# Rows turned by VectorE after a trip through HBM, in place of 296 TensorE transposes

## The chip, the cores and the metric

The kernel runs on one core of a Trainium2 chip. The metric is device microseconds (us) of one execution; lower is better. The kernel before takes 2199.61 us, the median of three runs (2198.78 to 2200.4).

## The reference, cut to what matters

The input is 1250 rows of 1024 values. Everything below is in fp32.

```python
xn = layernorm(x)                                    # no scale, no shift
u  = xn @ root + bias + sum_r mean_r(xn) @ weight[r]  # 8 relations, 40000 edges
z  = concat([u, xn]) @ w_gate + b_gate
h  = tanh(u) * z + xn * (1 - z)
q, k, v, g = xn @ Wq, xn @ Wk, xn @ Wv, sigmoid(xn @ Wg + bg)     # 16 heads of 64
o  = linear_attention(elu(q) + 1, elu(k) + 1, v) * g
x1 = x + h + o @ Wo
i, c, f = layernorm(x1) @ W_iT + b_i, ... @ W_cT + b_c, ... @ W_oT + b_o   # one LSTM step from zero
out = x1 + sigmoid(f) * tanh(sigmoid(i) * tanh(c))
```

Four matrices of 1250 x 1024 serve as the left factor of products and are needed with their columns on the partitions: `xn`, `o`, `u` and `layernorm(x1)`, in this order.

## The kernel before, in words

The rows are cut into ten tiles of 128 (the last has 98). A product by one half (512 columns) of a weight matrix is a *stage*, one tile of it a *unit* (`UNIT`, `STAGE`, `place`): 24 matmuls, eight steps `k` over the contraction by three, since each operand is split into a high part (fp32r) and the rest. The stages in order are 16 of `weight` (Y), then R, V, K, X, G, Q, O, C and the three of the last layer (I, T, F), mostly two of each. Units are named here as C1,4: stage C, half 1, tile 4. In the first two stages tiles alternate between the halves, so tile t (up to 5) is wanted at unit 2t. Q has 12 units of another shape a half, O, C and I ten.

Nothing is scheduled automatically. Each of the five engines has one program written in order, a loop over the units `q` and the steps `k`, with semaphores between them. What an engine's code does "at step k of unit q" stands in that place of its own queue; a wait there holds back everything after it on that engine. The SyncE queue (SP) issues all the loads and stores that are named here. Its loop for unit q begins while TensorE is at unit q-1, since it ends with `store_unit(q-1)`, which waits until the result of unit q-1 is out of PSUM. There are three accumulators (`acc`): unit q can't begin before the result of q-3 is taken (by ScalarE in Y and V, by VectorE's `evict`, `elu_high` or `make_x1` elsewhere). In stage Q TensorE also waits, at step 5 of each unit, for VectorE's `elu_high` of the unit before (`read_out`).

A left factor is turned tile by tile beside the products. For `xn`, `turn_x` at the units of `TURN_AT`; for `o`, `turn_o` at `TURN_O_AT`; for `u`, `turn_u` two units behind O1; for `layernorm(x1)`, `turn_x1` three units behind C1. Each is eight TensorE transposes of 128 x 128 into the PSUM tile `tp` at k = 2 (L821; tile 0 of x by L829), then at k = 4 ScalarE's copy to the high part `aThi` (L991) and at k = 5 VectorE's subtraction to `aTlo` (L1148). The tile must be there when the first stage that uses it comes to it.

`ln_x` normalizes a tile of x on VectorE (L1155 to L1170) at the units of `LN_AT`; GpSimd's `rows_sum` adds it to x (L1671); SP stores both (`xn_d`, `xs_d`, L726, L728), and loads the next tile of x into the place that falls free (`next_x`, L520), four places in all. In C1, `make_x1` (L1519 to L1530) makes a tile of x1 and its sums, ScalarE takes the root, `scale_x1` makes the scale, and ScalarE's `normalize_x1` (L1036) writes the normalized halves to `A` and `lnb`.

Of the kernel before, what the change touches and what calls it, by code (L numbers as in the profile page):

```python
# [199 lines left out]
def build(nc, x, src, dst, edge_type, weight, root, bias, w_gate, b_gate, Wq, Wk, Wv, Wg, bg, Wo,  # L200
          W_iT, b_i, W_oT, b_o, W_cT, b_c, out):
    with ExitStack() as ctx:
# [308 lines left out]
        def _(sp):  # L511
# [1340 lines left out]
```

## Time and profile before

| | before |
|---|---|
| median of 3 runs | 2199.61 us |
| profiled execution | 2199.8 us, of which span 2198.0 us |
| TensorE (PE) busy | 2182.2 us, 99% of the span |
| VectorE (DVE) busy | 1177.1 us, 54% |
| ScalarE (ACT) / GpSimd (POOL) busy | 439.9 us / 718.6 us |
| chain that ended last | PE 98%, of it L821 (transposes) 1% and L968 90% |
| granted TensorE clock | full, in all 40 slices |
| DMA | 416.62 MB, mean 190 GB/s |

The span is the time between the first and the last instruction. Matmuls overlap in the profile: one is shown as 0.39 to 0.40 us long while the next begins 0.23 us later, so starts are what to read.

### The profile page before, as it was taken

What the parts mean: (1) busy time and instruction counts of PE and PEld (TensorE: products, weight loads), DVE (VectorE), ACT (ScalarE), POOL (GpSimd) and SP (SyncE); (2) the same over time, 40 slices, a digit from 0 to 9 for tenths busy, and PEclk for the clock granted to TensorE, in tenths of its full rate; (3) what the DMA queues carried; (4) which work ended last, traced back from release to release, by engine and by line L of the source; (5) the groups of instructions that cost most, each with busy time, mean ns of one, the idle gap of its engine ahead of it and who ended that gap; (6) DMA issues with size and microseconds to landing.
All of it is one profiled execution on the core that took longest, in us unless ns stands there. A gap on an engine that the chain in (4) does not pass through costs nothing.

```text
span 2198.0 us, 25434 instructions
## 1 busy us (share of the span) xinstructions
PE 2182.2 (99%) x10042; PEld 1768.3 (80%) x10042; DVE 1177.1 (54%) x1605; ACT 439.9 (20%) x618; POOL 718.6 (33%) x597
## 2 busy tenths in 40 slices
PE   8999999999999999999999999999999999999999
PEld 6878888888888888888777787889988888888887
DVE  6331677726666566665765676653432367234233
ACT  3221111211111111100221200112321314121121
POOL 4103002055555555544655355521210453000000
PEclk9999999999999999999999999999999999999999
DMA  7543321456788988784968788853127885013102
GB/s 254 186 131 97 110 85 50 128 199 204 274 284 289 312 294 311 243 265 140 324 230 312 241 296 297 273 178 129 48 78 232 270 284 169 34 35 120 59 35 80
DMA packets 191266, 416.62 MB, mean 190 GB/s; under 512 B 33951, under 2 KB 44772, under 8 KB 191146
## 3 DMA queue, kind: packets, MB, share of 16 engines
q1 hardware_dynamic: 127946, 229.10, 30.8%
q0 software_dynamic: 63200, 185.89, 25.4%
q8 instruction: 79, 1.29, 0.2%
q14 instruction: 41, 0.34, 0.1%
HBM read 352.34 MB, written 103.66 MB: 207 GB/s over the span
## 4 chain that ended last, share of the span: by engine, by line
PE 98%; DVE 1%; DMA 0%; ACT 0%; issue 0%; DVEq 0%; ACTq 0%
PE acc L968 90%; PE acc L963 5%; PE tp L821 1%; PE agg L872 1%; PE misc L857 1%; DVE Wlo L1143 0%; DMA xr<-in_x 0%; PE agg L976 0%; PE acc L976 0%; DVE stats L1155 0%; PE tp L829 0%; PE misc L872 0%; DVE xnb L1170 0%; ACT L1012 0%; DVE aTlo L1148 0%
## 5 line engine op out<-in xcount | busy, mean ns | idle before, releaser
L968 PE MATMUL acc<-Whi,aThi 128*128 128x512 f32 (+1 forms) x2872 | 1138.1, 396 | 2.1 <-DVE Wlo L1143 1.6
L968 PE MATMUL acc<-Whi,aTlo 128*128 128x512 f32 (+1 forms) x2872 | 1131.8, 394 | 0.0
L968 PE MATMUL acc<-Wlo,aThi 128*128 128x512 f32 (+1 forms) x2872 | 1128.3, 393 | 0.0
L968 PEld LDWEIGHTS acc<-Whi,aTlo 128*128 128x128 f32 (+1 forms) x2872 | 532.6, 185 | 133.5
L968 PEld LDWEIGHTS acc<-Wlo,aThi 128*128 128x128 f32 (+1 forms) x2872 | 533.8, 186 | 130.9
L968 PEld LDWEIGHTS acc<-Whi,aThi 128*128 128x128 f32 (+1 forms) x2872 | 532.5, 185 | 132.4 <-DVE Wlo L1143 2.0
L1708 POOL DMA_INDIRECT ring<-y_d,edge x390 | 485.1, 1244 | 428.4 <-DVE U L1339 159.1
L1143 DVE TENSOR_TENSOR Wlo<-Wraw,Whi 128x1024 fp32r<-128x1024 f32 x152 | 186.8, 1232 | 322.3 <-ACT Whi L987 321.9
L999 ACT COPY res<-acc 128x512 f32<-128x512 f32 (+1 forms) x180 | 105.8, 588 | 833.8 <-PE acc L968 810.8
L1339 DVE SCALAR_TENSOR_TENSOR U<-ring,edge,U 128x1024 f32<-128x1024 f32 x180 | 230.3, 1280 | 23.2 <-DMA ring<-y_d,edge 22.8
L1339 DVE SCALAR_TENSOR_TENSOR odd<-ring,edge,odd 128x1024 f32<-128x1024 f32 x170 | 217.5, 1279 | 22.2 <-DMA ring<-y_d,edge 21.8
L987 ACT CAST Whi<-Wraw 128x1024 fp32r<-128x1024 f32 x152 | 158.5, 1046 | 196.2 <-DMA Wraw<-in_L_gnn_w_gate 71.9
L1469 DVE TENSOR_TENSOR res<-acc,bias_sb 128x512 f32<-128x512 f32 x99 | 68.5, 691 | 213.2 <-PE acc L968 123.4
L1695 POOL DMA_INDIRECT slot_d<-table,slot x20 | 21.8, 1088 | 227.9 <-DVEq L1299 222.4
L1045 ACT ACTIVATE res<-res 128x512 f32<-128x512 f32 (+1 forms) x59 | 37.3, 633 | 282.3 <-DVE res L1469 282.3
L1448 DVE SCALAR_TENSOR_TENSOR res<-acc,res 128x512 f32<-128x512 f32 (+3 forms) x44 | 28.0, 637 | 103.9 <-ACT res L1012 103.9
L1148 DVE TENSOR_TENSOR aTlo<-tp,aThi 128x1024 fp32r<-128x1024 f32 (+1 forms) x39 | 46.7, 1198 | 53.7 <-ACT aThi L991 53.7
L963 PE MATMUL acc<-aThi,Whi 128*128 128x384 f32 (+1 forms) x192 | 69.9, 364 | 0.0
L1815 POOL TENSOR_TENSOR og<-og,part 128x384 f32<-128x384 f32 (+1 forms) x32 | 27.7, 876 | 127.8 <-DVE part L1499 127.8
L963 PE MATMUL acc<-aThi,Wlo 128*128 128x384 f32 (+1 forms) x192 | 67.6, 352 | 0.0
L963 PE MATMUL acc<-aTlo,Whi 128*128 128x384 f32 (+1 forms) x192 | 67.5, 352 | 0.0
L1010 ACT ACTIVATE res<-acc 128x512 f32<-128x512 f32 (+3 forms) x44 | 24.5, 556 | 181.2 <-PE acc L968 93.0
(177 smaller groups left out, 1034.8 us busy)
## 6 DMA issues: line engine op xcount, KB each, us to landing
y_d<-res SPq DMA_DIRECT2D x144, 256.0 KB
Wraw<-in_L_gnn_weight SPq DMA_DIRECT2D x64, 512.0 KB, 5.5
Wraw<-in_L_gnn_w_gate SPq DMA_DIRECT2D x16, 512.0 KB, 6.0
ring<-y_d,edge POOLq DMA_INDIRECT x390, 6.3
xr<-in_x SPq DMA_DIRECT2D x9, 512.0 KB, 4.5
xn_d<-xnb SPq DMA_DIRECT2D x9, 512.0 KB, 5.6
xs_d<-xr SPq DMA_DIRECT2D x9, 512.0 KB, 5.6
ur_d<-res SPq DMA_DIRECT2D x18, 256.0 KB
```

Source lines behind the costliest of these rows:

```text
L963: mm = nc.tensor.matmul(to, a[:, s % 2, k, cols], b[:, k, c0:c0 + w], start=start, stop=stop)
L968: mm = nc.tensor.matmul(to, a[:, k, rows(i)], b[:, s % 2, k, :], start=start, stop=stop)
L987: nc.scalar.copy(granule(Whi, n), granule(Wraw, n)).then_inc(w_hi, 1)
L999: nc.scalar.copy(res[0:width(i), q % 3, :], acc[0:width(i), q % 3, :]).then_inc(evac_a, 1)
L1045: nc.scalar.activation(a, a, ACT.Tanh if kind == T_ else ACT.Sigmoid).then_inc(gate_act, 1)
L1143: nc.vector.tensor_tensor(granule(Wlo, n), granule(Wraw, n), granule(Whi, n).bitcast(F32), ALU.subtract).then_inc(w_lo, 1)
L1148: nc.vector.tensor_tensor(aTlo[:, :, rows(t)], turned_rows(width(t)), aThi[:, :, rows(t)].bitcast(F32), ALU.subtract).then_inc(done, 1)
L1339: nc.vector.scalar_tensor_tensor(to, g, scale, to, ALU.mult, ALU.add).then_inc(u_acc, 1)
L1448: nc.vector.scalar_tensor_tensor(a, p, 0.0, a, ALU.max, ALU.add).then_inc(evac_v, 1)
L1469: nc.vector.tensor_tensor(to, p, bias_sb[0:w, n % 2, :], ALU.add).then_inc(evac_v, 1)
L1708: pool.indirect_dma_start(ring[:, j % RING, :], None, a, bass.IndirectOffsetOnAxis(ap=index, axis=0), bounds_check=top - 1, oob_is_err=Fal ...
L1815: nc.gpsimd.tensor_tensor(o, o, part[0:w, a % 2, n, :], ALU.mult).then_inc(gated, 1)
```

## The change

The transposes of `o`, `u`, `layernorm(x1)` and of tiles 3 to 9 of `xn` leave TensorE. The rows are stored to HBM and read back by quarters: partition 32a + n gets, of the rows n, n+32, n+64, n+96 of the tile, the columns of quarter a (256 of them). VectorE's transpose of 32 x 32 blocks then gives 128 columns on the partitions, in another order of the contraction than before; the host stores the weights in the same order. `aTraw`, the target, lies over `aTlo`, and is subtracted in place.

- `load_quarters`: a tile is 4 loads of 128 KB in pieces of 1 KB, 8 loads for the last tile. It serves `xn` (`load_z`), `o` (`load_o`), `u` (`load_u`), `layernorm(x1)` (`load_x1n`), and `xn` again for tanh(u) (`load_tx`). `store_th` stores by quarters.
- New stores: `store_o` (three groups of tiles), `store_x1n` (two halves a tile). `xn` was stored before.
- VectorE: `turn_quarters` at k = 2 or 3, one instruction a tile (two for the last), and `rows_sum` in place of GpSimd's; for tiles 0 to 2, which TensorE still turns, a copy ahead of it.
- The places: `LN_AT`, `TURN_AT`, `XS_AT`, `NEXT_X_AT`; `turn_u` one unit behind, `turn_x1` four.

```diff
-LN_AT = {1: 2, 2: 3, 4: 4, 6: 5, 7: 6, 8: 7, 9: 8, 10: 9}
-TURN_AT = {1: 1, 3: 2, 5: 3, 7: 4, 8: 5, 9: 6, 10: 7, 11: 8, 12: 9}
+LN_AT = {1: 2, 2: 3, 5: 4, 6: 5, 7: 6, 8: 7, 10: 8, 11: 9}
+TURN_AT = {1: 1, 3: 2, 5: 3, 7: 4, 8: 5, 9: 6, 10: 7, 12: 8, 13: 9}
+TURNED_BY_PE = 3
+XS_AT = {4: (0,), 5: (1, 2, 3), 6: (4,), 7: (5,), 8: (6,), 9: (7,), 11: (8,), 12: (9,)}
+NEXT_X_AT = {5: (0,), 6: (1, 2, 3), 8: (4,), 9: (5,)}
-TURN_O_AT = {place(Q_, 1, 6 + t): t for t in range(3)}
-TURN_O_AT |= {place(Q_, 1, 10): 3, place(Q_, 1, 11): 4, place(O_, 0, 0): 5}
-TURN_O_AT |= {place(O_, 0, t - 4): t for t in range(6, T)}
+TURN_O_AT = {place(Q_, 1, 7 + t): t for t in range(3)}
+TURN_O_AT |= {place(Q_, 1, 11): 3, place(O_, 0, 0): 4, place(O_, 0, 1): 5}
+TURN_O_AT |= {place(O_, 0, t - 3): t for t in range(6, T)}
+STORE_O_AT = {place(Q_, 1, 6): 0, place(Q_, 1, 10): 1, place(O_, 0, 2): 2}
+        aTraw = at(top[0] - up(4 * K * N), "aTraw", [128, K, N])
         def u_turn(q):
-            return turn_at(O_, 1, 2, q)
+            return turn_at(O_, 1, 1, q)
+        def x1_norm(q):
+            return turn_at(C_, 1, 1, q)
         def x1_turn(q):
-            return turn_at(C_, 1, 3, q)
+            return turn_at(C_, 1, 4, q)
+            def load_quarters(to, of, t, done):
+                for a in range(4):
+                    part = to[32 * a:32 * a + 32, :].rearrange("p (m f) -> p m f", f=QUARTER)
+                    cols = slice(a * QUARTER, (a + 1) * QUARTER)
+                    if t < T - 1:
+                        sp.dma_start(part, blocks(of[rows(t), cols])).then_inc(done, 16)
...
+            def load_z(t):
+                sp.wait_ge(xn_st[t % XS], 16 * (t // XS + 1))
...
+                load_quarters(zx[:, t % 2, :], xn_d, t, z_in[t % 2])
+            def store_o(g):
+                sp.wait_ge(gated, reads_to(12 + 4 * g + 3))
+                sp.dma_start(o_d[g * 384:g * 384 + 384, :].rearrange("(t p) n -> p t n", p=128), og[:, 3 * g:3 * g + 3, :]
+                             ).then_inc(rows_st, 16)
...
+            def load_o(g):
+                sp.wait_ge(rows_st, 16 * (4 if g == 2 else g + 1))
+                if g:
+                    sp.wait_ge(o_turned, 3 * g)
+                for t in group_tiles(g):
+                    load_quarters(og[:, t, :], o_d, t, o_in)
+            def store_x1n(t):
+                sp.wait_ge(ln2_done, 2 * (t + 1))
...
+            def load_x1n(t):
+                sp.wait_ge(rows_st, 16 * 4 + 32 * (t + 1))
...
+                load_quarters(zx1[:, t % 2, :], x1n_d, t, z_in[t % 2])
             for q in range(UNITS + 1):
+                if LN_AT.get(q - 2, 0) >= TURNED_BY_PE:
+                    load_z(LN_AT[q - 2])
+                if LN_AT.get(q - 1, 0) >= TURNED_BY_PE:
+                    store_xn(LN_AT[q - 1])
+                for t in XS_AT.get(q, ()):
+                    if t < TURNED_BY_PE:
+                        store_xn(t)
+                    store_xs(t)
+                for t in NEXT_X_AT.get(q, ()):
+                    next_x(t)
...
                     store_unit(q - 1)
...
+                if x1_norm(q - 3) is not None:
+                    load_x1n(x1_norm(q - 3))
+                if x1_norm(q - 2) is not None:
+                    store_x1n(x1_norm(q - 2))
+            def turn_quarters(of, t, done):
+                of = of.rearrange("p (m j f) -> p j m f", m=4, f=32)
+                if t < T - 1:
+                    nc.vector.transpose(aTraw[:, :, rows(t)], of).then_inc(done, 1)
...
+            def turn_o(t):
+                g = min(t // 3, 2)
+                dve.wait_ge(o_in, 16 * sum(quarter_transfers(p) for p in range(group_tiles(g).stop)))
+                dve.wait_ge(prod, place(Q_, 1, 4 * g + 3) + 1)
+                turn_quarters(og[:, t, :], t, o_turned)
```

Three places show how the work moved. The first is VectorE in the early units, tiles 3 and 4 of x: before, from the high part of tile 2 on (`tp` is the PSUM tile).

```order
L1148 TENSOR_TENSOR aTlo<-tp,aThi 128x8x128 [waits x_hi]
L1155 BN_STATS stats<-xr 128x6 [waits x_in0]
...
L1170 TENSOR_SCALAR xnb<-xr,stats 128x1024 [waits xs_made,x_turned,xn_st0,dve_step]
L1148 TENSOR_TENSOR aTlo<-tp,aThi 128x8x128 [waits x_hi]
L1155 BN_STATS stats<-xr 128x6 [waits x_in1]
```

The same place now (`zx` holds the quarters of xn):

```order
L1297 TENSOR_TENSOR xr<-xr,xnb 128x1024 [waits ln_done]
L1303 BN_STATS stats<-xr 128x6 [waits x_in0]
...
L1317 TENSOR_SCALAR xnb<-xr,stats 128x1024 [waits xs_made,xn_st0,dve_step]
L1297 TENSOR_TENSOR xr<-xr,xnb 128x1024 [waits ln_done]
L1266 STREAM_TRANSPOSE aTraw<-zx 128x8x128 [waits z_in1]
L1260 TENSOR_TENSOR aTlo<-aTraw,aThi 128x8x128 [waits x_hi]
L1303 BN_STATS stats<-xr 128x6 [waits x_in1]
```

Before, the transposes of tile 3 stood on TensorE; now the turn of tile 3 stands on VectorE behind the normalization of tile 4, which waits for the load of tile 4 of x (`x_in0`).

The second place is SP in the same units, now:

```order
L832 DMA xn_d<-xnb 128x1024 [waits ln_done]
L624 DMA y_d<-res 128x512 [waits evac_a]
L574 DMA zx<-xn_d 32x4x256 [waits xs_made,x_turned,xn_st3]
L574 DMA zx<-xn_d 32x4x256 x3
L832 DMA xn_d<-xnb 128x1024 [waits xs_made]
L837 DMA xs_d<-xr 128x1024 [waits xs_made]
...
L837 DMA xs_d<-xr 128x1024 [waits xs_made] x2
L567 DMA xr<-in_x 128x1024 [waits xs_st0]
L624 DMA y_d<-res 128x512 [waits evac_a]
L832 DMA xn_d<-xnb 128x1024 [waits ln_done]
L837 DMA xs_d<-xr 128x1024 [waits xs_made]
L567 DMA xr<-in_x 128x1024 [waits xs_st1]
```

The first load of `xr` is that of tile 4, behind six stores of rows and the quarters of tile 3; the load of tile 5 stands behind the store of the normalized tile 4.

The third place is SP in C1, now (`zx_139` is the buffer `zx1`, `x_d` the array of x1):

```order
L748 DMA cring<-base_d 128x512
L624 DMA x_d<-res 128x512 [waits x1_made]
L574 DMA zx_139<-x1n_d 32x4x256 [waits x1_turned,rows_st]
L574 DMA zx_139<-x1n_d 32x4x256 x3
L756 DMA x1n_d<-A 128x512 [waits ln2_done]
L757 DMA x1n_d<-lnb 128x512
L748 DMA cring<-th_d 128x512 [waits res_st2,x1_made]
```

The quarters of one tile are loaded behind the store of the unit's x1 (`x1_made`), so behind VectorE's work on the same unit. VectorE there, now:

```order
L1673 TENSOR_TENSOR res<-acc,cring 128x512 [waits p_made,prod,ln2_done,res_st0]
L1675 TENSOR_TENSOR res<-res,cring 128x512 [waits evac_v]
L1677 BN_STATS x_stats<-res 128x6 [waits x1_made]
...
L1266 STREAM_TRANSPOSE aTraw<-zx_139 128x8x128 [waits prod,z_in0]
L1690 RECIPROCAL x_scale<-x_scale 128x1 [waits ln2_root]
...
L1260 TENSOR_TENSOR aTlo<-aTraw,aThi 128x8x128 [waits x1_hi]
L1673 TENSOR_TENSOR res<-acc,cring 128x512 [waits p_made,prod,ln2_done,res_st1]
```

One unit's result is taken (L1673), then the transpose waits for the quarters (`z_in0`), the scale for ScalarE's root, the subtraction for ScalarE's high part, and only then is the next result taken. ScalarE in the same units, now:

```order
L1135 ACTIVATE lnb<-res,x_scale 128x512 [waits x1_turned,ln2_ready]
L1135 ACTIVATE A<-A,x_scale 128x512
L1122 ACTIVATE x_scale<-x_scale 128x1 [waits ln2_var]
L1091 CAST aThi<-aTraw 128x8x128 [waits x1_turned]
L1135 ACTIVATE lnb<-res,x_scale 128x512 [waits x1_turned,ln2_ready]
```

The rows are the same as before in kind, but the turn that `normalize_x1` (L1135) of tile t waits for, that of tile t-2, now stands one unit behind it in VectorE's queue; before it stood in TensorE's queue, in the unit of the normalization itself.

## Rows read from the trace of the kernel before

**Rows 1.** Page, busy time: engine, us, share of the span, instructions.

```profile
PE 2182.2 (99%) x10042; PEld 1768.3 (80%) x10042; DVE 1177.1 (54%) x1605; ACT 439.9 (20%) x618; POOL 718.6 (33%) x597
```

**Rows 2.** Chain that ended last, around the last turn of o: start, us, what.

```profile
1635.22 0.88 PE tp L821 x8
...
1641.66 0.87 PE tp L821 x8
1642.54 5.57 PE acc L968 x24
1648.11 0.68 PE tp L821 x8
```

**Rows 3.** Groups by line: busy us, mean ns, idle before.

```profile
L821 PE MATMUL tp<-ident,A 128*128 128x128 f32 x36 | 5.4, 273 | 0.8 <-DVE aTlo L1148 0.8
```

**Rows 4.** Timeline of TensorE, turn of tile 3 of x: start, us.

```profile
44.91 1.03 PE L821 MATMUL tp<-ident,xnb 128*128 128x128 f32 x8
```

**Rows 5.** Timeline of VectorE, early units; in brackets idle us before, releaser.

```profile
30.58 1.28 DVE L1170 TENSOR_SCALAR xnb<-xr,stats 128x1024 f32<-128x1024 f32 x1
41.40 1.29 DVE L1155 BATCH_NORM_STATS2 stats<-xr 128x6 f32<-128x512 f32 x2 [5.16 <-DMA xr<-in_x]
44.23 0.81 DVE L1170 TENSOR_SCALAR xnb<-xr,stats 128x1024 f32<-128x1024 f32 x1
```

**Rows 6.** Timeline of SP's queue, early units.

```profile
36.77 0.43 SPq L520 DMA_DIRECT2D xr<-in_x  x1
40.71 0.50 SPq L728 DMA_DIRECT2D xs_d<-xr  x1
47.50 0.33 SPq L520 DMA_DIRECT2D xr<-in_x  x1
57.12 0.46 SPq L728 DMA_DIRECT2D xs_d<-xr  x1
62.12 0.33 SPq L520 DMA_DIRECT2D xr<-in_x  x1
```

**Rows 7.** A window in O1: us, engines busy, clock, DMA share, GB/s.

```profile
1700.00:1720.00 20.00, 20.00 (x102) 16.54 (x101) 8.01 (x8) 6.86 (x7) 7.19 (x3) 1.00 0.96 345
```

**Rows 8.** The loads of V in pieces of 512 bytes, by tile.

```profile
L565 SPq DMA_DIRECT2D vld<-v_d x20: 348/360/605, 1073.3 to 1252.0; - x20
...
DMA to landing us min/median/max: 2.8/3.8/6.9
```

**Rows 9.** Page, groups: VectorE's pass over 1024 values in SBUF.

```profile
L1143 DVE TENSOR_TENSOR Wlo<-Wraw,Whi 128x1024 fp32r<-128x1024 f32 x152 | 186.8, 1232 | 322.3 <-ACT Whi L987 321.9
```

**Rows 10.** Timelines of GpSimd, ScalarE and VectorE in Q1.

```profile
1570.67 1.01 POOL L1815 TENSOR_TENSOR og<-og,part 128x384 f32<-128x384 f32 x1 [3.86 <-DVE part L1499]
1581.89 0.49 ACT L1010 ACTIVATE res<-acc 128x384 f32<-128x384 f32 x1 [2.82 <-PE acc L963]
1583.04 0.56 DVE L1448 SCALAR_TENSOR_TENSOR res<-acc,res 128x384 f32<-128x384 f32 x1 [1.64 <-ACT res L1012]
1586.45 0.56 DVE L1499 TENSOR_TENSOR part<-agg,rden 128x384 f32<-128x384 f32 x1
```

**Rows 11.** Timeline of VectorE, first result of C0.

```profile
1753.41 0.69 DVE L1519 TENSOR_TENSOR A<-acc,cring 128x512 f32<-128x512 f32 x1 [10.95 <-POOL cring L1826]
```

**Rows 12.** Timelines of VectorE and ScalarE in C1.

```profile
1811.80 0.69 DVE L1519 TENSOR_TENSOR res<-acc,cring 128x512 f32<-128x512 f32 x1
1812.52 0.94 DVE L1521 TENSOR_TENSOR res<-res,cring 128x512 f32<-128x512 f32 x1
1818.97 1.16 DVE L1521 TENSOR_TENSOR res<-res,cring 128x512 f32<-128x512 f32 x1
...
1815.92 0.82 ACT L1036 ACTIVATE lnb<-res,x_scale 128x512 f32<-128x512 f32 x1 [0.16 <-DVE x_scale L1540]
1816.64 0.80 ACT L1036 ACTIVATE A<-A,x_scale 128x512 f32<-128x512 f32 x1
1821.43 1.03 ACT L987 CAST Whi<-Wraw 128x1024 fp32r<-128x1024 f32 x1
1822.37 1.01 ACT L991 CAST aThi<-tp 128x1024 fp32r<-128x1024 f32 x1
```

More of the change, by code:

```diff
@@ L367, in build @@
             sem(n) for n in ("ln_var", "ln_root", "ln_done", "xs_made", "x_turned", "x_hi", "x_lo"))
+        z_in = [sem(f"z_in{i}") for i in range(2)]
+        z_turned = sem("z_turned")
+        rows_st = sem("rows_st")
+        o_in = sem("o_in")
         edges_in, edges_made, tail_made, codes_st, samples_in = (
@@ L441, in with_halves, with quarter_transfers, quarters_in, x_quarters_in @@
             return t + 2
+        def quarter_transfers(t):
+            return 8 if t == T - 1 else 4
+        def quarters_in(t, places):
+            return 16 * sum(quarter_transfers(p) for p in range(t % places, t + 1, places))
+        def x_quarters_in(t):
+            return 16 * sum(quarter_transfers(p) for p in range(t, TURNED_BY_PE - 1, -2))
+        def blocks(a):
+            return a.rearrange("(m n) f -> n m f", n=32)
         def x_tiles(i):
@@ L638, in store_th @@
                     wait_th_stored(sp, t - TH_SEMS)
-                sp.dma_start(th_d[rows(t), :], uio[t][0:width(t), :]).then_inc(th_st[t % TH_SEMS], 16)
+                done = th_st[t % TH_SEMS]
+                for a in range(4):
+                    part = uio[t][32 * a:32 * a + 32, :].rearrange("p (m f) -> p m f", f=QUARTER)
+                    cols = slice(a * QUARTER, (a + 1) * QUARTER)
+                    if t < T - 1:
+                        sp.dma_start(blocks(th_d[rows(t), cols]), part).then_inc(done, 16)
+                    else:
+                        sp.dma_start(blocks(th_d[t * 128:t * 128 + 96, cols]), part[:, 0:3, :]).then_inc(done, 16)
+                        rest = N - t * 128 - 96
+                        sp.dma_start(th_d[N - rest:N, cols],
+                                     uio[t][32 * a + 32 - rest:32 * a + 32, 3 * QUARTER:4 * QUARTER]).then_inc(done, 16)
             def load_u(t):
@@ L834, in turn_x @@
                 pe.wait_ge(x_lo, with_halves(t - 1))
[L835 removed]
+                for j in range(K):
+                    tr = turn_step(t, j)
+                tr.then_inc(x_turned, 1)
             def any_bad():
@@ new lines, in turn_x1, with rows_sum @@
+            def turn_x1(t):
+                dve.wait_ge(z_in[t % 2], x_quarters_in(T - 2 + t % 2) + quarters_in(t, 2))
+                dve.wait_ge(prod, place(C_, 1, t) + 1)
+                turn_quarters(zx1[:, t % 2, :], t, x1_turned)
+            def rows_sum(t):
+                dve.wait_ge(ln_done, with_halves(t))
+                if t < TURNED_BY_PE:
+                    chain(nc.vector.tensor_copy(by_quarters(xnb[:, t, :]), by_steps(zx[:, t % 2, :])))
+                a = xr[0:width(t), t % XS, :]
+                nc.vector.tensor_tensor(a, a, xnb[0:width(t), t % XS, :], ALU.add).then_inc(xs_made, 1)
@@ L1599, in _ @@
                         continue
+                    if k == 2 and TURNED_BY_PE <= TURN_AT.get(q, 0):
+                        turn_x(TURN_AT[q])
                     if k == 4 and q in TURN_AT:
-                        lo_turned(TURN_AT[q], x_hi, with_halves(TURN_AT[q]), x_lo)
-                    if k == (4 if q == 1 else 0) and q in LN_AT:
+                        lo_x(TURN_AT[q])
+                    if k == 4 and q == 1:
+                        rows_sum(0)
+                    if k == (4 if q in (1, 8, 10) else 0) and q in LN_AT:
                         ln_x(LN_AT[q])
+                        if q >= 3:
+                            rows_sum(LN_AT[q])
+                    if k == 4 and q == 3:
+                        for t in range(1, 4):
+                            rows_sum(t)
                     if q == 17 and k == 6:
```

198 lines of the change are left out of this document (113 added, 85 removed).

## The prediction, made before the changed kernel was run

> **What bounds the kernel now.** I read the page first: TensorE is busy 99% of the span [rows 1], at full clock in all slices, so only what shortens or delays TensorE's own queue counts. The chain of waits shows what the change can win: a unit of 24 matmuls takes 5.57 us, and where a tile is turned, 0.87 or 0.88 us stand between two such pieces, 0.68 for the last tile of 98 rows [rows 2]. Then I read the engines that come in for TensorE, place by place: VectorE and SP's queue in the early units [rows 4 to 6], VectorE and GpSimd in Q1 and C0 [rows 10, 11], VectorE and ScalarE in C1 [rows 12]. VectorE's 54% says little here: what matters is how long one of its instructions waits for a transfer while results that TensorE needs taken stand behind it.
>
> **What is removed.** 37 turns leave TensorE: 33 of full tiles at 0.87 and four of last tiles at 0.68, 28.7 + 2.7 = 31.4 us, and 0.8 us in which it waited for VectorE before a turn of x1 [rows 2, 3]. Sum: -32.2 us. Nothing covers this time now, so it is won wholly, if nothing else comes late.
>
> **Prices of what is added.** SP's issue of a load or store: 0.33 to 0.50 us [rows 6], taken as 0.45. From the issue of a 512 KB store to the wait behind it: 5.0 us (57.12 to 62.12) and 6.8 us (40.71 to 47.50). From the issue of a load of x to its use: 4.6 us (36.77 to 41.40) [rows 5, 6]. For a load of 128 KB there is no row; the nearest are 256 KB loads in pieces of 512 bytes, 2.8 to 3.8 us [rows 8], bounded below by the data alone at 345 GB/s, 0.4 us [rows 7]. I take 3.3. VectorE's transpose of 1024 columns isn't in the trace: its nearest passes are 0.81 us (one operand) and 1.23 us (two) [rows 5, 9]; I take 1.2, with 0.8 and twice the longer one, 2.45, as ends. ScalarE's high part stays at 1.0 us [rows 12].
>
> On transfers the Trainium skill has a rule, in "DMA: Bandwidth & Descriptors", § Anatomy of one DMA: about 2.0 us fixed and the bytes at 436 GB/s, as fitted for GpSimd's path. As an estimate by it a quarter lands after 2.3 us, 1.0 sooner than the value I take, so that each of some eight steps of C1 would be 1 us shorter and the sum 8 us smaller; the rows of V contradict it, with a least value of 2.8 us. On the transpose "VectorE: DVE Perf Modes", § The three transpose paths, gives 311 ns for 128 x 128 in bf16; eight of them would be an estimated 2.5 us a tile, for which I have no row.
>
> **The early units.** Tile 3 of x is wanted at unit 6. TensorE gets there at 44.91 + 0.87 + 18 x 0.232 = 49.96 before [rows 4], so at 49.1 without the turn. VectorE's queue now has: normalize tile 4, add it to x, turn tile 3. Tile 4 needs its load, and that stands in SP's queue behind a chain: tile 3 is normalized at 31.9 before [rows 5], now 2.0 later for the copy and the sum of tile 0 (0.8 + 1.2), 33.9; its store lands 5.0 later, 38.9; then four quarters and a store, and `xs_d` of tile 0, to 41.1; that lands at 46.1; the load issued then takes 4.6 if alone, 50.7. It isn't alone: quarters, stores of rows and units that are issued between 39 and 46 make 4.5 MB, at 345 GB/s 13 us, to 52; with the load's own 1.5 us and 2 of landing 55.5. I take 54 between 50.7 and 55.5. From there: normalize 41.40 to 45.04, 3.6 us [rows 5], sum 1.2, turn 1.2, high part 1.1, low part 1.2, together 8.3, to 62.3 against 49.1: +13.2 (10 to 15).
>
> Tile 4 is wanted two units later, 62.3 + 11.1 = 73.4. The load of tile 5 is issued when tile 4 is normalized and summed, 54 + 3.6 + 1.2 and three issues, 60; it lands at 64.6; two tiles are normalized and summed in VectorE's queue ahead of this turn (2 x 4.8), then 3.5 for turn, high and low part: 77.7, so +4.3 (0 to 6). Tiles 8 and 9 have the same pattern with a unit or two of reserve; +1.5 (0 to 3.5). Early units: +19 (10 to 25).
>
> **Q1 and O0.** The first group of o is complete at 1571.7 [rows 10]. Its store is 1.5 MB: 5.0 to 6.8 for the first third and 2.9 for the rest at 345 GB/s, 8.5, to 1580.2. Then 12 quarters: 11 issues of 0.45 and 3.3, to 1588.4. VectorE comes to the turn at 1583.6 - 0.9 = 1582.7 and waits 5.7 us. Behind it stand high and low part, `attend` (1.0) and the `elu_high` of Q1,7: 1588.4 + 1.2 + 1.1 + 1.2 + 1.0 + 0.6 = 1593.5. TensorE wants that at step 5 of Q1,8, which begins at 1581.9 - 0.9 + 4.9 = 1585.9, so at 1589.2: +4.3. I count 3.5, since the middle of the store's row is a guess, and as much again for the second and third group together, whose turns meet SP's queue in the same state, but behind a unit more. +7 (2 to 12).
>
> **C0.** The first result of C0 is taken 10.95 us late already [rows 11], and the next of its kind would stop TensorE 2 us later. It hangs on the last tile of tanh(u), whose load is now eight transfers behind four stores by quarters. No turn is left to give it time: +2 (0 to 4).
>
> **C1.** From C1,4 on, VectorE takes a result and adds (0.7 and 0.7 to 1.2 [rows 12], 1.6); SP stores x1 and issues four quarters (0.37 + 3 x 0.45 to the last issue, then 3.3: 5.0); turn 1.2; ScalarE normalizes the tile that waits for this turn (0.72 + 0.80), takes the root (0.2) and makes the high part (1.0, with 0.9 for a weight's in every other unit) [rows 12], 2.7 and 0.45 on average; low part 1.15. That is 12.1 us a step where a unit is 5.57. If the bn sums and the scale fall wholly into these waits nothing is added for them. Counted from below (landing 2.8, adding 0.7, no weight) it is 10.9; I take 11.3, nearer the lower end, because the first tiles' normalizations wait for no turn. TensorE, three accumulators ahead, needs the result of C1,9 at the start of I0,2: after 6 steps and 0.7, 68.5, where 8 units are 44.6: +23.9. The next takes a step more and a unit, +5.7. Then the steps have no x1 to make, but tile 7's rows are stored one step late: +4. C1 and I0: +34 (22 to 45).
>
> Work that moved and costs nothing: GpSimd's sums ran beside all else, and VectorE's ten (12 us) are paid in the early chain alone, where I counted them; quarters of u are loaded up to six tiles ahead. In O1 SP has 14 issues (6.3 us) in a unit of 5.57 for four units, 3 us of arrears that `xs` and stores, two units ahead, cover. The DMA share there is 0.96 already [rows 7], and the same bytes in pieces of 1 KB keep the rate only if a piece costs no more than its bytes; no row shows that, and a rival below has it.
>
> **Sum.** -32.2 + 19 + 7 + 2 + 34 = +29.8. The profiled execution took 2199.8 us, so 2229.6; the median of the runs is 0.2 lower: 2229.4 us. By ends: -32.2 + 34 = 2201.4 and -32.2 + 86 = 2253.4.
>
> **Rivals.** *All rows come in time.* For it: TensorE is the one bound, VectorE is idle 46% of the span, and there are three accumulators. It decides if a step of C1 is under (44.6 - 0.7)/6 = 7.3 us and tile 4 of x lands by 41 as before. Then 2199.6 - 32.2 = 2167.4. Against it: a store and a load in series alone are 10 us in the early chain, and 5 of each step are SP's queue and one landing. 6 in 100, with all below 2190.
>
> *The lower ends hold together*, stores landing in 5.0 and quarters in 2.8 wherever they are waited for: 2190 to 2212, centre 2201. 12 in 100.
>
> *VectorE's transpose is slow or small pieces are.* A transpose of 2.45 adds 1.25 in about 13 places on the path (two early, three in Q and O, eight in C1): +16, 2245. If pieces of 1 KB also take more of the DMA engines' time, O1, full now, falls behind, and quarters land later in every chain. 2248 to 2280, 20 in 100.
>
> **How the numbers follow.** The forecast has 62 in 100, with a range of its own of 2212 to 2248. To hold 8 in 10 I take in part of the slow rival and the lower end's upper half: 2206 to 2262. A measurement can tell about 0.2% (4.4 us) from no change. Faster: the first rival's 0.06 and 0.02 of the second. Same: 0.03. Slower: 0.89.
>
> **What would show each step.** No transposes of og, uio, A and lnb on TensorE, and units of 5.57 us there. TensorE idle some 13 us before unit 6 and some 4 before unit 8, released by VectorE's `aTlo`; VectorE idle there on the load of x, and in C1 on the quarters, with results taken 11 us apart for six units; TensorE idle 5 to 6 us before each of several units of C1 and I0. If VectorE shows no wait on the quarters in C1 longer than 2 us, or x's tile 4 lands before 45, the forecast is wrong. So it is if the transposes are far from 1.2 us.

## The result, and the profile after

| | before | after |
|---|---|---|
| median | 2199.69 us (4 runs) | 2268.73 us (4 runs, 2263.67 to 2270.41) |
| profiled execution, its span | 2199.8, 2198.0 us | 2263.67, 2261.8 us |
| TensorE busy | 99% [rows 1] | 96% |

The ratio is 1.031, with a 95% interval of 1.0292 to 1.0328: 69.0 us slower, where +29.8 was forecast. The direction was right, the time lies 6.7 us above the range. The profiled run was the quickest of its four, so everything below is accounted in its span, 63.8 us over that of before. The four runs lie 6.7 us apart, so between two versions of this kernel a difference of 4 us or less in the medians says little by itself.

The page of the changed kernel, with TensorE in 40 slices and the clock granted to it in tenths:

```profile
PE 2174.2 (96%) x9746; PEld 1753.2 (78%) x9746; DVE 1233.8 (55%) x1659; ACT 440.1 (19%) x618; POOL 698.6 (31%) x587
...
PE   6899999999999999999999999999999795899999
...
PEclk9899999999999999999999999999999897999999
```

296 transposes have left (10042 - 9746), and TensorE is below 9 tenths in a few slices: early, in slice 31 (C0), in 33 and 34 (C1). The clock, full everywhere before, drops in three of the same slices (slices are counted from 0). TensorE's waits, in total, times and longest:

```profile
PE acc L1061 <- DVE res L1673: 23.1, 5, 8.2
PE acc L1061 <- DVE A L1673: 16.9, 1, 16.9
PE acc L1061 <- DVE aTlo L1260: 16.6, 3, 13.8
PE acc L1061 <- DVE Wlo L1238: 6.7, 2, 5.2
PE acc L1061 <- DVE A L1623: 4.6, 2, 4.1
PE agg L994 <- DVE res L1602: 3.7, 3, 2.9
PE acc L1061 <- DVE res L1616: 2.5, 1, 2.5
```

L1260 is the early units (0.8 us on ScalarE besides), L1602 and L1616 are Q1 and O0 (0.8 us of them is not counted below; 0.6 of that stood early in Q before, too), `A L1673` is C0, the rest C1 and I0 (of the 6.7 us of Wlo 1.5 stand in unit 1). The stretches at the lower clock, as windows: length, TensorE's busy us, and after the other engines the granted clock, DMA share and GB/s:

```profile
51.50:68.60 17.10, 5.65 (x13) 4.47 (x14) 10.25 (x22) 1.93 (x4) 0.00 (x0) 0.50 0.70 234
...
1768.40:1785.50 17.10, 3.99 (x9) 3.15 (x10) 4.10 (x6) 1.04 (x1) 11.50 (x8) 0.50 0.61 186
...
sum 78.50, PE 43.02 PEld 33.69 DVE 44.19 ACT 12.58 POOL 20.75; mean PE 3.91 PEld 3.06 DVE 4.02 ACT 1.14 POOL 1.89
```

There are eleven of them, each during or right after a wait. In them TensorE works 43.0 us at 0.50, the 1.2 GHz level, so 21.5 us more than at 2.4 GHz. Waits and this loss by place (the forecast's term behind it): early 17.4 + 4.5 = 21.9 (19); Q1 and O0 5.4 + 3.2 = 8.6 (7); C0 16.9 + 2.0 = 18.9 (2); C1 and I0 32.9 + 11.7 = 44.6 (34). Less the 32.2 us removed that is +61.8; 2.0 us are in no place. The miss in the span is 34.0 us, of which C0 has 16.9 and C1 with I0 10.6.

**Early units.** TensorE, VectorE, then SP's queue:

```profile
62.95 0.77 PE L1061 MATMUL acc<-Whi,aThi 128*128 128x512 f32 x1 [13.78 <-DVE aTlo L1260]
```

```profile
54.42 1.29 DVE L1303 BATCH_NORM_STATS2 stats<-xr 128x6 f32<-128x512 f32 x2 [13.37 <-DMA xr<-in_x]
...
59.23 1.24 DVE L1266 STREAM_TRANSPOSE aTraw<-zx 128x1024 f32<-128x1024 f32 x1
```

```profile
41.90 1.20 SPq L832 DMA_DIRECT2D xn_d<-xnb  x1
43.14 1.12 SPq L837 DMA_DIRECT2D xs_d<-xr  x1
...
48.03 1.20 SPq L567 DMA_DIRECT2D xr<-in_x  x1
```

Tile 4 is used at 54.4 (forecast 54, against 41.4 in [rows 5]), and unit 6 begins at 62.95 (62.3). The chain is the forecast's.

**O1 and C0.** In O1 and C0 a loop runs beside TensorE: GpSimd subtracts xn from tanh(u) (L1977), SP stores the result and then loads the rows of xn for the tile after next. The window in O1, to be held against [rows 7]; then the subtractions, SP's stores and loads between them, and TensorE's wait:

```profile
1705.00:1725.00 20.00, 20.00 (x88) 16.25 (x87) 13.28 (x13) 8.55 (x9) 4.32 (x2) 1.00 1.07 288
```

```profile
1704.35 2.48 POOL L1977 TENSOR_TENSOR uio<-uio,tx 128x1024 f32<-128x1024 f32 x1 [63.44 <-ACT uio L1116]
1710.30 2.48 POOL L1977 TENSOR_TENSOR uio<-uio,tx 128x1024 f32<-128x1024 f32 x1 [3.47 <-ACT uio L1116]
1727.17 2.40 POOL L1977 TENSOR_TENSOR uio<-uio,tx 128x1024 f32<-128x1024 f32 x1 [14.39 <-DMA tx<-xn_d]
...
1775.78 2.34 POOL L1977 TENSOR_TENSOR uio<-uio,tx 128x1024 f32<-128x1024 f32 x1 [5.36 <-DMA tx<-xn_d]
```

```profile
1716.88 2.36 SPq L724 DMA_DIRECT2D th_d<-uio  x4
1719.28 1.89 SPq L574 DMA_DIRECT2D tx<-xn_d  x4
...
1724.16 2.69 SPq L724 DMA_DIRECT2D th_d<-uio  x4
```

```profile
1781.51 0.80 PE L1061 MATMUL acc<-Whi,aThi 128*128 128x512 f32 x1 [16.87 <-DVE A L1673]
```

The DMA engines are full, at 288 GB/s instead of 345. SP's round of a unit takes 7.3 us (1716.88 to 1724.16) where the unit is 5.57. The subtractions from the third to the tenth come (1775.78 - 1727.17) / 7 = 6.9 us apart, all waiting for rows. Before, they were 6.4 apart:

```profile
1722.99 2.42 POOL L1820 TENSOR_TENSOR uio<-uio,tx 128x1024 f32<-128x1024 f32 x1 [4.08 <-ACT uio L1017]
1729.40 2.40 POOL L1820 TENSOR_TENSOR uio<-uio,tx 128x1024 f32<-128x1024 f32 x1 [4.00 <-ACT uio L1017]
```

That is a unit with its turn, 5.57 + 0.87, and all subtractions but the third waited for ScalarE's tanh, so for TensorE's pace. Now the unit is shorter, the loop's round is longer, and TensorE runs ahead of it: seven rounds are 9.6 us longer than seven units. More is lost before the rounds begin. The third subtraction comes 16.9 us after the second (1710.30 to 1727.17), 11.3 us more than a unit. The change turns u a unit sooner, so the first subtraction comes a unit sooner too, but the loop still starts at O1,4: the load of the third tile's rows is issued at 1719.28, 12.5 us after the first subtraction's end (1706.83).

**C1.** VectorE takes results (L1673), turns x1 (L1266) and, in some steps, makes a weight's low part (L1238). Then SP's queue at one step:

```profile
1861.45 0.68 DVE L1673 TENSOR_TENSOR res<-acc,cring 128x512 f32<-128x512 f32 x1
...
1873.65 0.68 DVE L1673 TENSOR_TENSOR res<-acc,cring 128x512 f32<-128x512 f32 x1
...
1880.77 1.25 DVE L1266 STREAM_TRANSPOSE aTraw<-zx 128x1024 f32<-128x1024 f32 x1 [4.20 <-DMA zx<-x1n_d]
...
1884.69 2.31 DVE L1238 TENSOR_TENSOR Wlo<-Wraw,Whi 128x1024 fp32r<-128x1024 f32 x1
1886.92 2.28 DVE L1260 TENSOR_TENSOR aTlo<-aTraw,aThi 128x1024 fp32r<-128x1024 f32 x1
1889.12 0.68 DVE L1673 TENSOR_TENSOR res<-acc,cring 128x512 f32<-128x512 f32 x1
...
1900.39 0.68 DVE L1673 TENSOR_TENSOR res<-acc,cring 128x512 f32<-128x512 f32 x1
...
1913.30 0.68 DVE L1673 TENSOR_TENSOR res<-acc,cring 128x512 f32<-128x512 f32 x1
```

```profile
1875.44 0.32 SPq L624 DMA_DIRECT2D x_d<-res  x1
1875.85 1.81 SPq L574 DMA_DIRECT2D zx<-x1n_d  x4
```

A step without a weight is 12.2 us (1861.45 to 1873.65), one with a weight 15.5 (to 1889.12); the next two are 11.3 and 12.9. The results of C1,3 and C1,9, six steps apart:

```profile
1844.85 0.69 DVE L1673 TENSOR_TENSOR res<-acc,cring 128x512 f32<-128x512 f32 x1 [1.44 <-PE acc L1061]
...
1924.63 0.68 DVE L1673 TENSOR_TENSOR res<-acc,cring 98x512 f32<-98x512 f32 x1
```

79.8 us, where 6 x 11.3 = 67.8 were forecast. The six are 16.6, 12.2, 15.5, 11.3, 12.9 and 11.3 us: of the 12.0 us too many 11.1 stand in the three steps with a weight, and the last two short steps are as forecast.

### The profile page after: what moved, and what is told of

It is laid out like the page before. It is cut to its first block, busy times and chain, and to the rows that moved or that the text cites. A ratio compares the mean times of both kernels' runs of the same rounds, so it can differ in the third digit from the quotient of the medians.

```text
span 2261.8 us, 25108 instructions
## 1 busy us (share of the span) xinstructions
PE 2174.2 (96%) x9746; PEld 1753.2 (78%) x9746; DVE 1233.8 (55%) x1659; ACT 440.1 (19%) x618; POOL 698.6 (31%) x587
## 4 chain that ended last, share of the span: by engine, by line
PE 79%; DMA 5%; issue 5%; DVE 4%; SPq 4%; POOL 1%; ACT 1%; DVEq 0%; POOLq 0%; ACTq 0%
PE acc L1061 78%; SPq L574 2%; DMA zx<-x1n_d 1%; DMA bias_sb<-xs_d 1%; POOL og L1973 1%; DVE aTraw L1266 1%; DMA o_d<-og 1%; SPq L724 1%; PE misc L979 1%; DMA xr<-in_x 0%; DVE aTlo L1260 0%; DMA og<-o_d 0%; DMA x1n_d<-lnb 0%; DVE Wlo L1238 0%; SPq L624 0%
## 5 line engine op out<-in xcount | busy, mean ns | idle before, releaser
L1238 DVE TENSOR_TENSOR Wlo<-Wraw,Whi 128x1024 fp32r<-128x1024 f32 x152 | 188.1, 1241 | 297.9 <-ACT Whi L1080 297.4
L1602 DVE SCALAR_TENSOR_TENSOR res<-acc,res 128x512 f32<-128x512 f32 (+3 forms) x44 | 28.0, 636 | 98.2 <-ACT res L1112 98.2
L1851 POOL DMA_INDIRECT runs<-code_d,run_row x20 | 21.0, 1052 | 164.7 <-DVEq L1349 158.9
L1091 ACT CAST aThi<-aTraw 128x1024 fp32r<-128x1024 f32 (+1 forms) x37 | 38.0, 1027 | 138.0 <-DVE aTraw L1266 123.5
```

The source lines that it names most:

```text
L1091: nc.scalar.copy(aThi[:, :, rows(t)], aTraw[:, :, rows(t)]).then_inc(done, 1)
L1238: nc.vector.tensor_tensor(granule(Wlo, n), granule(Wraw, n), granule(Whi, n).bitcast(F32), ALU.subtract).then_inc(w_lo, 1)
```

## The experiments

**One part undone at a time.** Each kernel is the changed one with one of its four parts as before, with the weights' rows in the order that fits. For x1, for instance (x, o and u alike):

```diff
+                if k == 2 and x1_turn(q) is not None:
+                    turn_x1(x1_turn(q))           # eight transposes on TensorE, out of A and lnb
-                if x1_norm(q - 3) is not None:
-                    load_x1n(x1_norm(q - 3))
-                if x1_norm(q - 2) is not None:
-                    store_x1n(x1_norm(q - 2))
```

> The changed kernel with the part on x undone: all ten tiles of x are turned by TensorE, GpSimd makes their sums, LN_AT, TURN_AT and SP's order in the first units are those of before. Theory (each part costs what stands at its place): TensorE lost 17.4 us idle and up to 4.5 us at the lower clock before and in units 6 to 14; 7 turns come back, 5.9 us: 2268.7 - 21.9 + 5.9 = 2252.7. If the time at the lower clock was hidden by the waits that followed it, about 2 us less is won: 2255. Rival (early delays are caught up by slack later): no slack is left, so nothing of the kind; a time of 2268 or more would show it.

> The changed kernel with the part on o undone: o is turned by TensorE out of og, with no store and reload. Theory: 5.4 us idle and 3.4 us at the lower clock go, 10 turns of 8.5 us come back: 2268.4, no change. Rival (stores and quarters of o put SP's queue so late that O1 and the start of C0 pay for it): the 16.9 us wait at C0 falls as well, to about 2255 to 2262.

> The changed kernel with the part on u undone: u, xn for tanh(u) - xn, and the stores of that are moved in whole rows, u is turned by TensorE. Theory (quarters of u, tx and th make O1 late and that is what TensorE waits for at the start of C0): of the 16.9 us idle and 2.0 us at the lower clock there at most 1 us stays, 10 turns of 8.5 us come back: 2258 to 2260. Rival (the arrears come from the stores and quarters of o ahead of it): the wait at C0 stays over 8 us and the time is 2268 to 2277.

> The changed kernel with the part on x1 undone: x1 is turned by TensorE out of A and lnb. Theory: all 32.9 us idle and 11.7 us at the lower clock in C1 and I0 go, 10 turns of 8.5 us and the 0.8 us of before come back: 2268.7 - 44.6 + 9.3 = 2233.4. Rival (a part of the waits in C1 is the late C0 handed on): 2240 to 2250.

Measured: 2250.2 without the part on x, 2261.0 without o, 2256.8 without u, 2226.9 without x1. So the parts cost 18.5, 7.7, 12.0 and 41.9 us net of the turns they save. Each is a loss, and x1's is by far the largest. The spans of the profiled executions (2247.6, 2257.8, 2256.8 and 2226.1, against 2261.8) give 14.2, 4.0, 5.0 and 35.7. The medians sum to 80 where 69 were lost, the spans to 59 where 63.8 were, so whether the parts share waits is not shown. x1's 35.7 is what the waits at its place gave, 44.6 - 9.3; the 2233.4 expected for a4 took them off the median, 5 us over the profiled run, and so came out 6.5 too high. In a3 the wait for `A L1673` at C0 is gone altogether, so it comes from the part on u; in a2 it is somewhat smaller, as the rival had it, but stays:

```profile
PE acc L1070 <- DVE A L1693: 13.6, 1, 13.6
```

In a1 and a4 it stays at 17.4 and 18.7, so neither the early delay nor x1 has to do with it. In b2 and d1 below, which leave O1 as it is, it is 16.4 and 17.6: a change of 2 us in this wait is within what differs from one profile to the next.

**Does the lower clock cost its 21.5 us?**

```diff
+                for _ in range(FED.get(q, 0)):    # 96 at unit 6, 128 at C0,3, 20 to 48 at C1,8 to I0,3
+                    nc.tensor.transpose(tp[:, 0, 0:128], ident[:, :], ident[:, :])
```

> The changed kernel; ahead of eight units that wait TensorE first makes transposes of the identity into a free accumulator, nothing reads them: 96 before unit 6, 128 before C0,3, and 40, 48, 20, 32, 28 and 24 before C1,8 to I0,3, each batch shorter than the wait that stands there (0.109 us apiece). Theory H (the lower clock after a wait is mostly hidden, since another engine sets when the next unit may begin): only the 2.0 us after C0's wait and 1 to 3 us at the ends of the early and the last group of waits are won, 2263 to 2267, though the granted clock rises. Theory S (each microsecond at the lower clock costs half of itself, 21.7 in sum): 2248 to 2254. If the clock doesn't rise, neither is tested: 2268.7.

Measured: 2267.6 us, 1.1 less than the changed kernel, with a mean granted clock of 0.992 instead of 0.982 (a mean of 0.982 is 3.6% of the span at 0.5, 0.992 is 1.6%). Less was put to the test than Theory S had counted on: TensorE's busy time at the lower clock fell from 43.0 to 31.3 us, not to nothing. By Theory S that is 5.8 us, 2262.9. The four runs lie from 2265.9 to 2271.3, those of the changed kernel from 2263.7 to 2270.4; the times are against it, but do not settle it alone. Unit 6 begins 0.5 us sooner than in the changed kernel, and C0,3 0.1:

```profile
62.42 0.47 PE L1066 MATMUL acc<-Whi,aThi 128*128 128x512 f32 x1 [2.70 <-DVE aTlo L1265]
...
1781.37 0.80 PE L1066 MATMUL acc<-Whi,aThi 128*128 128x512 f32 x1 [3.87 <-DVE A L1678]
```

Between the two, early in Q, this kernel is 2.5 us ahead (1504.25 against 1506.75 for the first matmul there that waits for a result), and by C0,3 the lead is gone. In a chain that another engine paces, a slow unit mostly shortens the next wait. Two of the batches in I0 run on after their accumulator is free (32 transposes from 1918.95 to 1923.37, its result taken at 1918.29), so C1 and I0 are a poorer test than the places above. The Trainium skill, in "TensorE: Matmul & The Clock Gate", § HAM oscillation — how this bites in real kernels, counts half of the throttled time as penalty. An estimate by it, for stretches at the lower clock of 34.1 us instead of 78.5, is 22 us back; the run shows 1.1. The loss counted beside the waits above is therefore mostly part of what VectorE's and SP's chains cost, not a cause of its own.

**C1: the order in SP's queue.**

```diff
+                if x1_norm(q - 3) is not None:
+                    load_x1n(x1_norm(q - 3))
                 if q:
                     store_unit(q - 1)
-                if x1_norm(q - 3) is not None:
-                    load_x1n(x1_norm(q - 3))
```

> The changed kernel with one move in SP's queue: the quarters of x1's rows are loaded ahead of the store of the unit before, not behind it. Theory (a step of C1 runs result, store issued behind it, four quarters, landing, transpose; the reload waits for a result it doesn't need): the loop loses 1.4 us of VectorE, SP's issues and most of the landing, a step falls from 12.2 to 15 us to 6 to 10, and of the 44.6 us at C1 and I0 some 15 to 25 stay: 2240 to 2250. Rival (the rows' store has not landed any sooner, and its landing holds the step): over 2262.

Measured: 2245.0 us, 23.7 less. VectorE's results in C1:

```profile
1861.88 0.68 DVE L1673 TENSOR_TENSOR res<-acc,cring 128x512 f32<-128x512 f32 x1
...
1869.80 0.68 DVE L1673 TENSOR_TENSOR res<-acc,cring 128x512 f32<-128x512 f32 x1
...
1881.07 0.68 DVE L1673 TENSOR_TENSOR res<-acc,cring 128x512 f32<-128x512 f32 x1
```

A step is 7.9 us without a weight and 11.3 with one. The reload stood behind the store of a result that it doesn't need; that alone was half of x1's loss or somewhat more (23.7 of 41.9 us by the medians, 18.4 of 35.7 by the spans).

**C1: the long steps.**

```diff
+            if STAGE[s][0] == C_ and STAGE[s][2] == 1:      # weights of I0 at C1,2 to C1,5
+                n = GRAN * (s + 1) + i - 2
+                return range(n, n + 1) if i in (2, 3, 4, 5) else range(0)
```

> The changed kernel; the high and low parts of I0's weights are made at C1,2 to C1,5 instead of C1,2, 4, 6 and 8. Theory W (the loop of C1 takes 12.2 us a step, and 14.6 to 15 where ScalarE's 1.0 and VectorE's 1.2 to 2.3 us for a weight stand in it; the prediction had 0.45 for them): two of the three long steps become short ones and the time falls by 3 to 7 us, to 2262 to 2266. Rival (the weights fall into the wait for the rows and cost nothing; the long steps come from the transfers): 2267 to 2270.

Measured: 2264.6 us, 4.1 less. The results:

```profile
1879.95 0.68 DVE L1676 TENSOR_TENSOR res<-acc,cring 128x512 f32<-128x512 f32 x1
...
1891.79 0.68 DVE L1676 TENSOR_TENSOR res<-acc,cring 128x512 f32<-128x512 f32 x1
...
1903.41 0.68 DVE L1676 TENSOR_TENSOR res<-acc,cring 128x512 f32<-128x512 f32 x1
```

Where no weight is left in the loop a step takes 11.8 and 11.6 us, near the forecast's 11.3. The first two steps still have one each, and from C1,3 to C1,9 the six take 78.3 us instead of 79.8. The time is at the edge of what these runs tell apart; the steps are not.

**O1 and C0: pieces, or the queue?** b3 moves the same bytes in as many transfers, each of 32 whole rows, so the values of u no longer fit the order of the weights; b4 issues u's quarters from ScalarE:

```diff
-                load_quarters(uio[t], u_d, t, u_in[t % U_SEMS])
+                load_by_rows(uio[t], u_d, t, u_in[t % U_SEMS])          # b3; tx and th alike
+                load_quarters(uio[t], u_d, t, u_in[t % U_SEMS], act)    # b4
```

> The changed kernel with u, xn for tanh(u) - xn and the stores of tanh(u) - xn moved in the same number of transfers of the same bytes, but each of 32 whole rows of 4 KB instead of pieces of 1 KB; so u is put into the turned matrix in a wrong order, which changes the values and no time. Theory D (pieces of 1 KB take the DMA engines more time: share 1.02 at 267 GB/s): the 16.9 us wait at C0 falls under 6 and the time is 2255 to 2261. Theory Q (SP's queue, 14 issues and 7.3 to 7.8 us in a unit of 5.57, is what is late): the wait stays within 3 us of 16.9 and the time is 2265 to 2271.

> The changed kernel with the quarters of u issued by ScalarE's queue instead of SP's; pieces and bytes are the same. Theory Q (SP's queue): 4 of its 14 issues a unit are gone, it keeps up with 5.57 us, the wait at C0 falls under 6: 2255 to 2261. Theory D (pieces of 1 KB): the wait stays within 3 us, 2265 to 2271; somewhat longer if the loads of u, now sooner, push others back.

Measured: 2264.3 and 2261.7 us. TensorE's wait in b3 and in b4:

```profile
PE acc L1068 <- DVE A L1680: 15.3, 1, 15.3
```

```profile
PE acc L1047 <- DVE A L1674: 12.0, 1, 12.0
```

Neither theory holds by itself. In b3 the wait is 1.6 us shorter, less than the 2 us by which it differs between profiles, and the time 4.4. But b3 is a weak test of small pieces: its transfers cover 32 partitions each as before, and in them the engines moved no more (281 GB/s, the last row of this document). What pieces of 1 KB cost in this loop stays open. In b4 the wait is 4.9 us shorter, and the rounds of the loop fall from 6.9 to 6.3 us (third subtraction at 1726.34, tenth at 1770.62). The Trainium skill, in "DMA: Bandwidth & Descriptors", § Issuing engines are not separate DMA queues, has a second issuing engine save the issue time alone, "usually small relative to the DMA itself". That fits: what left SP is the issue of four loads, 1.89 us a tile in the rows of O1, but in a loop that SP serves in series it is not small.

**O1 and C0: where the loop starts, and its order.** c1 moves stores and loads one unit forward, c2 does that and what b4 does, d2 puts the loads first:

```diff
-                    t = q - place(O_, 1, 4)
+                    t = q - place(O_, 1, 3)       # c1 and c2
-                        store_th(t)               # d2
                         if t + 2 < T:
                             load_tx(t + 2)
+                        store_th(t)
```

> The changed kernel; SP's store of tanh(u) - xn and its load of the rows for the tile after next come one unit sooner in its queue (from O1,3 on instead of O1,4). Theory L (the loop of load, subtraction and store starts late: the third subtraction waits 14.4 us for rows whose load is issued 12.5 us after the first subtraction's end): the wait at C0 falls by up to 5.6 us, 16.9 to 11 to 13, and the time to 2263 to 2265. Rival (SP's queue and the DMA engines are full, so a sooner start is used up by the fifth tile): wait still over 15.5, 2267 to 2270.

> The changed kernel with the move of c1_th_sooner, and u's quarters issued by ScalarE's queue (alone that gave 2261.7). If the two causes are apart, the gains add: 7.0 and 4 to 5, 2256 to 2258, wait at C0 6 to 8. Rival (the same microseconds, since the DMA engines at a share of 1.0 to 1.1 set the pace): 2260 to 2263.

> The changed kernel; in SP's queue the four loads of xn for tile t + 2 stand ahead of the four stores of tanh(u) - xn of tile t, not behind them, with the wait on the same subtraction. Theory C (the wait at C0 is the end of the loop subtraction, stores 1.8 to 2.7 us, loads 1.9, landing, subtraction): each step is 1.8 us or more shorter where it waits for the rows, the wait falls from 16.9 to 8 to 13, 2260 to 2265. Rival (the DMA engines at a share of 1.02 to 1.11 set the pace, so order moves nothing): 2267 to 2270.

Measured: 2258.9, 2255.7 and 2265.6 us. The wait in c1 and in c2 (in d2 it is 15.2 us):

```profile
PE acc L1061 <- DVE A L1673: 10.1, 1, 10.1
```

```profile
PE acc L1047 <- DVE A L1674: 7.6, 1, 7.6
```

A start one unit sooner is worth 6.8 us of wait and 9.9 of time, more than Theory L had; the third subtraction comes at 1722.66, 4.5 us sooner, and the rounds stay at 6.8 us. c2 adds up less than fully (13.0 against 9.9 + 7.0). Loads first give 3.1 us and 1.7 of wait, neither clear of what runs and profiles differ by; Theory C was too high.

**A version that keeps what pays.** From before, the parts on o and u only; o's turns a unit later; u's quarters from ScalarE, stores and loads of the loop a unit sooner; c4 adds x1 with b2's order, later turns, and d1's weights; d3 is c3 with d2's order.

```diff
-TURN_O_AT = {place(Q_, 1, 7 + t): t for t in range(3)}
-TURN_O_AT |= {place(Q_, 1, 11): 3, place(O_, 0, 0): 4, place(O_, 0, 1): 5}
-TURN_O_AT |= {place(O_, 0, t - 3): t for t in range(6, T)}
+TURN_O_AT = {place(Q_, 1, 8 + t): t for t in range(3)}
+TURN_O_AT |= {place(O_, 0, t - 3): t for t in range(3, 6)}
+TURN_O_AT |= {place(O_, 0, t - 2): t for t in range(6, T)}
```

> The kernel before with the parts on o and u alone; o's tiles are turned one unit later than in the changed kernel (the first at Q1,8), u as in c2_act_th. x and x1 are turned by TensorE. Theory: 20 turns leave TensorE, 17.2 us; the three waits of o are gone, since a turn stands a unit further behind its rows; at C0 up to 6 us of wait stay: 2182 to 2188. Rival (stores and quarters of o bring the queue late into O1 as in the changed kernel, and C0 waits 10 or more): 2192 to 2199.

> As c3_ou_act, with x1 turned by VectorE too: its rows are loaded ahead of the store of the unit before, its turns come a unit later (C1,5 to I0,4), a normalization waits for the load of the tile two before instead of its turn, and the weights of I0 are split at C1,2 to C1,5. Theory: 10 more turns and 0.8 us leave, 9.3 us, and 4 to 9 us of waits stay in C1 and I0 of the 44.6: the same as c3_ou_act within 4 us, or up to 5 us faster. Rival (store and reload of 512 KB, 10 us and more, hold each second tile whatever the order): 10 to 25 us slower than c3_ou_act.

> As c3_ou_act (2191.8), with the order of d2_tx_first. Theory C: of the 5.2 us wait at C0 at most 2 stay: 2187 to 2190. Rival (engines full): 2190 to 2193.

Measured: c3 2191.8 us, 0.9966 of before (0.9952 to 0.9980); c4 2198.0, 0.9992 (0.9983 to 1.0001); d3 2189.5, 0.9962 (0.9949 to 0.9976). d3 is 0.4% faster than before and 3.5% faster than the changed kernel. Its 2.3 us under c3 are not told apart by the times (c3 ran from 2190.8 to 2193.4, d3 from 2188.4 to 2192.7). Its waits at O0 and C0, where those of c3 were 1.8 and 5.2 us:

```profile
PE acc L1023 <- DVE aTlo L1224: 2.0, 1, 2.0
PE acc L1023 <- DVE A L1619: 1.9, 1, 1.9
```

No wait in Q1 is left that before did not have. Around both waits the clock is low for some 3.4 us each, as windows of d3:

```profile
1640.00:1655.00 15.00, 13.00 (x50) 10.16 (x49) 11.27 (x12) 4.10 (x4) 0.00 (x0) 0.89 0.56 181
1735.00:1760.00 25.00, 23.11 (x93) 18.34 (x92) 9.00 (x12) 3.15 (x3) 13.86 (x9) 0.93 0.97 308
```

(15 x 0.11 x 2 = 3.3 and 25 x 0.07 x 2 = 3.5.) Half of them, 3.4 us, stands in the span. The sum of the spans: 20 turns are 17.0 us, and 1.5 us of waits of before are gone (0.7 in unit 1, 0.8 before a turn of x1); less waits of 3.9 and the clock's 3.4 that is 11.2, and 10.8 are measured (2198.0 to 2187.2). The sum says where the time is, not what a full clock would give back. After the second stretch no wait follows, so its 1.7 us should be lost for good; a faster unit after the first could have lengthened the wait at C0. No run tests either. By the medians d3 is 9.3 us faster (2198.78 in the same session). c3 lies above the forecast for it, between theory and rival. c4 is 6.2 us slower than c3, between its theory and its rival: even repaired, the part on x1 costs more than the 9.3 us it saves, 9.9 us of waits in C1 and I0, 2.8 more at C0 and 2.5 at the lower clock.

## Why the prediction came out as it did

- **Removed, -32.2:** right: with it and the waits the span's difference closes to 2.0 us, and d3's 20 turns close to 0.4 us at the same 0.87 and 0.68.
- **Prices:** the transpose was taken at 1.2 us and takes 1.24. The rival of a slow transpose is out. A quarter of x1 lands 3.0 us after its issue in the median (3.3 taken), of o 3.7, of x 4.3, of u 5.6.
- **Early units, +19 (10 to 25):** 21.9; a1 gives 24.4 by the medians and 20.1 by the spans, with the 5.9 us of turns given back. Right in place, order and near in size. The second wait was 1.8 us instead of 4.3, because unit 6 ran partly at the lower clock (5.6 us of it, so 2.8 us longer).
- **Q1 and O0, +7 (2 to 12):** 8.6. Right, and half in Q1 and half in O0 as worked out; VectorE's wait for the first group is 4.2 us (5.7 forecast), its longest, 14.2 us for `og`, is the third group's.
- **C0, +2 (0 to 4):** this step failed; it measured 18.9. It rests on another: "In O1 SP has 14 issues (6.3 us) in a unit of 5.57 for four units, 3 us of arrears that `xs` and stores, two units ahead, cover". A round of the queue took 7.3 us, not 6.3, since loads were issued at 0.47 us apiece (1.89 / 4) and stores at 0.59 (2.36 / 4); and the arrears were not of four units. They fall on the loads for the subtraction, which are not two units ahead but in a loop: subtraction, store, load, subtraction. Its rounds took 6.9 us to the end, 9.6 us over seven units, where the 0.87 us of turn a unit had kept pace before. And the loop began late, which the prediction doesn't mention: the change turned u a unit sooner and left the loop's start at O1,4, behind more issues, so that the third subtraction lost 11.3 us, of which c1 took 4.5 back. The prediction saw that "no turn is left to give it time" and still priced only the last tile's transfers. c1 (the start) and b4 (the rounds) each take a part of TensorE's wait away, 6.8 and 4.9 us, a3 all of it; b3 and d2 move it too little to tell. So the place of the loop and the number of issues in SP's queue are shown as causes. How much of the rest the full DMA engines have is open.
- **C1 and I0, +34 (22 to 45):** 44.6, the right mechanism, mis-sized. The step's short form was right (11.3 twice and 12.2 in the changed kernel, 11.6 and 11.8 in d1). A weight in the loop was counted with 0.45 us a step on average; the three steps with one were 5.3, 4.2 and 1.6 us over 11.3. ScalarE's high part of the weight takes 1.0 us and VectorE's low part 1.2, and the long ones pay besides for VectorE beside GpSimd: in the rows above, the low parts of the weight (1884.69) and of the rows (1886.92) take 2.3 us instead of 1.2, each with a pass of GpSimd that had begun before it (at 1884.65 and 1885.99). The x1 part undone (a4) gives 45.0 us for this place by the spans.
- **Rivals:** the one of small pieces, 2248 to 2280, has the time in it. Its slow transpose is refuted. Its small pieces are not: the engines did move less a second in O1, as it has it, but b3 doesn't isolate the size of the pieces, and no run says how much of the waits it made.

## What to carry to other kernels

When work is taken off the engine that bounds a kernel, every loop beside it gets less time a round. Look up the period of each such loop in the trace and compare it with the new, shorter unit, not with the old one. When one member of a loop is moved sooner, move the start of the others with it. Where rows go out to memory and come back, put the reload in the queue ahead of everything that waits for a result, and count each instruction that stands in the loop in the steps that have it, not as an average. Read a low clock together with what follows: where another wait comes, it costs little (1.1 us of the 5.8 that b1 put to the test); after the last one, half of it should be lost (1.7 us in d3, not tested).

## What the runs showed of the hardware

- VectorE's transpose of 128 x 1024 fp32 values in 32 x 32 blocks takes 1.24 us, as long as its pass over two operands [rows 9].
- SP issued plain stores of 512 KB at 1.12 to 1.20 us behind quarters and other stores (41.90 to 49.2), where those of [rows 6] took 0.46 and 0.50. The kernel before has such long issues too, a little later, where stores follow on each other (1.20 at 72.80).
- A pass of VectorE over two operands took 2.3 us instead of 1.2 where a pass of GpSimd over two operands had begun before it (VectorE at 1884.69 and GpSimd at 1884.65; three such passes of VectorE in C1).
- With pieces of 1 KB among them the DMA engines moved 288 GB/s at a share of 1.07; in pieces of 2 and 4 KB 345 at 0.96 [rows 7]. Transfers of 32 whole rows (b3) were no better, 281 at 1.00:

```profile
1705.00:1725.00 20.00, 20.00 (x88) 16.22 (x87) 13.61 (x14) 8.71 (x10) 2.56 (x2) 1.00 1.00 281
```
